# Second FFN of a three-block kernel: rows scaled by their gates as they leave PSUM, added into the residual by the scattering transfer, and one memory-to-memory copy to the output

## The chip, the cores and the metric

The kernel runs on one core of a Trainium2 chip. The metric is the device time of one execution in microseconds, lower is better. A core has TensorE (PE) for matrix products, VectorE (DVE), ScalarE (ACT) and GpSimd (POOL) for elementwise work, and SyncE (SP), which only issues DMAs here. ACT and POOL issue DMAs too. Each engine works through its own list of instructions in order; semaphores tie the lists together. Indirect DMAs, whose rows are picked by a list of row numbers, are issued by POOL, which describes each of their rows.

## The reference

A residual stream x of 2 x 2048 tokens with 256 numbers each passes through an FFN with experts, a Mamba block and the same FFN again:

```
x = L0_attn_x
x = x + 0.5 * _L0_ffn_ref(_layernorm(x, axis=-1), ...)
x = x + _L0_attn_ref(_layernorm(x, axis=-1), ...)
x = x + 0.5 * _L0_ffn_ref(_layernorm(x, axis=-1), ...)
```

The FFN sends each token to the 2 of 8 experts with the largest logits, and adds their outputs weighted by a softmax over these two:

```
logits = jnp.einsum('btd,ed->bte', x, router_w)
top_vals, top_idx = jax.lax.top_k(logits, K)
top_w = jax.nn.softmax(top_vals, axis=-1)
h = jnp.einsum('nd,edh->enh', xf, w1)
h = jnp.square(jax.nn.relu(h))
y = jnp.einsum('enh,ehd->end', h, w2)
y_sel = y[idx_f, jnp.arange(N)[:, None]]
out = jnp.einsum('nk,nkd->nd', w_f, y_sel)
```

Everything is float32; the expert's hidden width is 512.

## The kernel before

The program has three blocks one behind the other: `ffn_block` with `first=True`, `mamba_block`, and `ffn_block` with `first=False`. The Mamba block leaves the residual rows in the tensor `x2_d` and the normalised rows in `xn_d`, both in the chip's memory. Only the third block is changed.

**Routing.** The second FFN has TOK = 4096 tokens, T = 32 groups of P = 128. Every token goes to two experts (TOP = 2), so there are 8192 pairs of a token and an expert. They are sorted by expert, and each expert's part is filled up to a multiple of 128: NT = 72 tiles of 128 rows. DVE makes the tables in a chain of small instructions: `gates` (two weights per token, already halved, L774 and L775), `token_of` (for each row of each tile the token whose normalised row is read, L785), `row_of` (the row of `ys_d` to which the result goes, L788) and `expert_i` (the expert of each tile, L793). The filling rows of a tile go to spare rows behind the real ones (`spare`). `ys_d` has a row for each pair, so no two rows of any tiles meet. While the tables are made, SP loads the low parts of the weights from `lo_d` (L344).

**The tile loop.** For tile t: POOL gathers 128 rows of `xn_d` (L422, tile `xs`); PE turns them (L601), ACT and DVE split them into a high and a low part (L504, L800); PE multiplies by the first weights with three pairs of parts, six products of 512 columns (L613, `pH`); ACT applies the relu (L491); PE turns the result (L622, `pR`), ACT squares it (L497, L499), DVE makes its low part (L805); PE multiplies by the second weights, twelve products (L633, `pY`); DVE copies the 128 x 256 result to `y` (L811, printed as `xs`, since both lie in one tensor), and POOL scatters it to `ys_d` (L427). PE works ahead: in the step of tile t it multiplies tile t+2, turns the rows of tile t+3 and the hidden values of t+1, and then finishes t (`down`). There are NX = 8 buffers for gathered rows and 8 for results.

On POOL the order is: eight gathers, and then in step t the gather for tile t+8 (which waits until PE has turned tile t) and the scatter of tile t (which waits for DVE's copy of tile t):

```
for t in range(NT):
    if t + NX < NT:
        gather(t + NX)
    scatter(t)
```

**The end.** During the tiles SP loads the residual `x2_d` in eight pieces of 512 KB to a tensor in SBUF, `res` (L377; it is printed as `room`). When all scatters have landed, SP loads both rows of every token from `ys_d` (L384, sixteen loads of 512 KB, three buffers), DVE multiplies them by their gates and adds them to `res` (L851, 64 instructions of 128 x 256), and ACT stores the eight finished pieces (L532).

Of the kernel before, what the change touches and what calls it, by code (L numbers as in the profile page):

```python
# [15 lines left out]
P = 128  # L16
D = 256
# [148 lines left out]
def ffn_block(nc, c, keep, x, router_w, w1, w2, xn_d, ys_d, lo_d, out, first, tables=None, early=None):  # L166
# [13 lines left out]
    TOK = x.shape[0]  # L180
# [4 lines left out]
    with ExitStack() as ctx:  # L185
        def sb(name, shape, dt):
            return ctx.enter_context(nc.sbuf_tensor(name, shape, dt))
# [6 lines left out]
        def step(name, unit=1):  # L194
            return Step(sem(name), unit)
# [16 lines left out]
        scratch = Carved(tables if first else sb("room" + tag, [P, T * D], F32))  # L212
        res = None if first else scratch.tensor[:, :].rearrange("p (i d) -> p i d", d=D)
# [32 lines left out]
        er = [a.rearrange("p (r n d) -> p r n d", r=TOP, d=D) for a in (*(xs[:, u * EG * TOP:(u + 1) * EG * TOP, :].rearrange("p n d -> p (n d)") for u in range(2)), hs[:, :])]  # L246
        NE = len(er)
# [33 lines left out]
        e_loaded = [step(f"e_loaded{u}", 16 * TOP) for u in range(NE)]  # L281
        out_loaded, early_loaded, early_hi, early_split = (sem(n) for n in ("out_loaded", "early_loaded", "early_hi", "early_split"))
        res_loaded, e_stored = sem("res_loaded"), sem("e_stored")
        e_first, e_done = step("e_first"), step("e_done")
# [38 lines left out]
        def _(sp):  # L323
# [49 lines left out]
            if out is not None:  # L373
                sp.wait_ge(experts_known, 1)
                for n in range(T // EG):
                    sp.wait_ge(y_copied.sem, y_copied.done(n * NT // (T // EG)))
                    sp.dma_start(res[:, n * EG:(n + 1) * EG, :], tiles(x, n * EG * P)).then_inc(res_loaded, 16)  # L377
                for u in range(NX):
                    sp.wait_ge(scattered[u].sem, scattered[u].done(NT // NX - 1))
                for n in range(T // EG):  # L380
                    if n >= NE:
                        sp.wait_ge(e_done.sem, e_done.done((n - NE + 1) * EG - 1))
                    for k in range(TOP):
                        sp.dma_start(er[n % NE][:, k, :, :], tiles(ys_d, n * EG * P + (1 + k * T) * P)).then_inc(e_loaded[n % NE].sem, 16)  # L384

        @block.gpsimd
        def _(pool):
# [6 lines left out]
            pool.iota(spare[:, :], pattern=[[0, NT // NX], [P, NX]], base=(C + 1) * P, channel_multiplier=1,  # L394
# [30 lines left out]
            def scatter(t):  # L425
                pool.wait_ge(y_copied.sem, y_copied.done(t))
                pool.indirect_dma_start(out=ys_d, out_offset=bass.IndirectOffsetOnAxis(ap=row_of[:, t:t + 1], axis=0),  # L427
                                        in_=y[:, t % NX, :], in_offset=None).then_inc(scattered[t % NX].sem, 16)
# [3 lines left out]
            pool.wait_ge(routed, 2)  # L432
            for t in range(NT):
                if t + NX < NT:
                    gather(t + NX)
                scatter(t)
            for u in range(NX):
                pool.wait_ge(scattered[u].sem, scattered[u].done(NT // NX - 1))

        @block.scalar  # L440
        def _(act):
# [87 lines left out]
            if out is not None:  # L529
                for n in range(T // EG):  # L530
                    act.wait_ge(e_done.sem, e_done.done(n * EG + EG - 1))
                    act.dma_start(tiles(out, n * EG * P), res[:, n * EG:(n + 1) * EG, :]).then_inc(e_stored, 16)  # L532
                act.wait_ge(e_stored, 16 * (T // EG))

# [127 lines left out]
        def _(dve):  # L662
# [112 lines left out]
            link(dve.tensor_tensor(gates[:, T:2 * T], gates[:, 0:T], top[:, 3, :], ALU.mult))  # L775
            dve.wait_ge(oh_used.sem, oh_used.done(C // PC - 1))
# [8 lines left out]
            dve.tensor_scalar(token_of[:, :], row_t[:, :], TOK - 1, None, ALU.bitwise_and).then_inc(routed, 1)  # L785

            link(dve.scalar_tensor_tensor(row_f[:, 2, :], row_f[:, 0, :], 0.0, spare[:, :], ALU.is_equal, ALU.mult))
            dve.tensor_tensor(row_of[:, :], row_f[:, 0, :], row_f[:, 2, :], ALU.add).then_inc(routed, 1)  # L788
# [4 lines left out]
            dve.tensor_scalar(expert_i[:, :], expert_f[:, :], float(E - 1), float(WCOLS), ALU.min, ALU.mult).then_inc(experts_known, 1)  # L793

# [12 lines left out]
            def copy_y(t):  # L807
                dve.wait_ge(y_ready.sem, y_ready.done(t))
                if t >= NX:
                    dve.wait_ge(scattered[t % NX].sem, scattered[t % NX].done(t // NX - 1))  # L810
                dve.tensor_copy(y[:, t % NX, :], pY[t % 2][:, 0:D]).then_inc(y_copied.sem, 1)  # L811
# [27 lines left out]

            if out is not None:  # L840
                for s in (*e_loaded, e_first, e_done):
                    s.open(dve)
                dve.wait_ge(res_loaded, 16 * (T // EG))
                for n in range(T // EG):
                    dve.wait_ge(e_loaded[n % NE].sem, e_loaded[n % NE].done(n // NE))
                    for k in range(TOP):
                        for m in range(EG):
                            i = n * EG + m
                            if k > 0:
                                dve.wait_ge(e_first.sem, e_first.done(i))  # L850
                            dve.scalar_tensor_tensor(res[:, i, :], er[n % NE][:, k, m, :], gates[:, i + k * T:i + k * T + 1], res[:, i, :],  # L851
                                                     ALU.mult, ALU.add).then_inc((e_first, e_done)[k].sem, 1)
# [850 lines left out]
def program(nc, x, w_in, conv_w, conv_b, dt_bias, a_log, d_skip, norm_w, w_out, router_w, w1, w2, out):  # L1703

    with ExitStack() as ctx:
        batches, tokens = x.shape[0], x.shape[0] * x.shape[1]
        xf, of = x.rearrange("b t d -> (b t) d"), out.rearrange("b t d -> (b t) d")

        xn_d = nc.dram_tensor("xn_d", (tokens, D), F32, kind="Internal").ap()
        ys_d = nc.dram_tensor("ys_d", ((TOP * (tokens // P) + 1 + NX) * P, D), F32, kind="Internal").ap()  # L1710
        x2_d = nc.dram_tensor("x2_d", (tokens, D), F32, kind="Internal").ap()
        lo_d = nc.dram_tensor("lo_d", (2, P, E * WCOLS), F32, kind="Internal").ap()
        c = make_constants(nc, ctx)
        keep = make_keep(nc, ctx, tokens)
        build_constants(nc, c)
        with ExitStack() as mid:
            with nc.sbuf_tensor("room1", [P, 4 * WORDS], F32) as tables:
                pass
            early = early_weights(nc, mid, w_in, norm_w, w_out)
            ffn_block(nc, c, keep, xf, router_w, w1, w2, xn_d, ys_d, lo_d, None, True, tables, early)  # L1720
            mamba_block(nc, c, keep, early, xf, ys_d, conv_w, conv_b, dt_bias, a_log, d_skip, x2_d, xn_d, batches)
        ffn_block(nc, c, keep, x2_d, router_w, w1, w2, xn_d, ys_d, lo_d, of, False)
# [24 lines left out]
```

## Time and profile before

| | |
|---|---|
| time, median of 3 runs | 1263.86 us (1262.22 to 1272.66) |
| span of the profiled execution | 1265.8 us |
| PE busy over the span | 1050.3 us (83%) |
| DVE, ACT, POOL busy | 748.1, 605.8, 607.9 us |
| second FFN: tables | about 927 to 965 us |
| second FFN: tiles | about 965 to 1226 us |
| second FFN: combining and storing | about 1226 us to the end |

The span goes from the first to the last instruction of the profiled execution, and it is 1.9 us longer than the median time of the runs. Engines run side by side, so busy times don't add up to the span. What counts is which engine is waited for in a stretch. A row of the chain of waits gives what the program's end waited for, back in time. "Granted clock" is the share of TensorE's full clock that the chip's throttle let it have.

### The profile page before, as it was taken

The page shows a single profiled execution, that of the slowest core. Times are in us where ns is not written, and L with a number is a line of the kernel's source. Part 1 is how long each engine was busy: PE and PEld are TensorE (multiplying, and loading weights), DVE is VectorE, ACT ScalarE, POOL GpSimd, SP SyncE. Part 2 cuts the span into 40 slices and gives each one's busy share as a digit, 9 for nine tenths or more (in the row PEclk, how much of TensorE's full clock was granted, in tenths as well). Part 3 has the DMA queues.
Part 4 walks back from the last instruction along what each step waited for, and adds up shares of the span by engine and source line. Part 5 has one row for each costly group of instructions (what it writes and reads, how often), then busy time and mean ns, then how long its engine had stood idle before and what let it go on. Part 6 is the DMA issues. An engine that isn't in the chain of part 4 may idle for free. (4 is left out here: it accounts for less than half of the span.)

```text
span 1265.8 us, 21732 instructions
## 1 busy us (share of the span) xinstructions
PE 1050.3 (83%) x6532; PEld 870.1 (69%) x6532; DVE 748.1 (59%) x1614; ACT 605.8 (48%) x1560; POOL 607.9 (48%) x612
## 2 busy tenths in 40 slices
PE   3746999999965788989898888989836999999960
PEld 2745999999954556666676666657525999999950
DVE  5974444444427778677878786865355444444437
ACT  1323555555533455556555656565314555555530
POOL 6922555555531245354545454647502555555520
PEclk9997999999985598899989989999858999999985
DMA  7872222322313101111111110000061232222339
GB/s 227 276 294 74 76 76 76 99 76 76 76 59 93 38 30 43 42 42 42 43 42 42 43 38 17 27 17 21 22 279 38 88 97 92 94 95 91 100 117 327
DMA packets 73258, 112.20 MB, mean 89 GB/s; under 512 B 10680, under 2 KB 60352, under 8 KB 71872
## 3 DMA queue, kind: packets, MB, share of 16 engines
q1 hardware_dynamic: 48704, 60.48, 14.2%
q0 software_dynamic: 13824, 37.77, 9.3%
q10 hardware_dynamic: 10624, 12.58, 2.9%
q8 instruction: 61, 1.00, 0.3%
q14 instruction: 45, 0.37, 0.1%
HBM read 66.76 MB, written 44.04 MB: 88 GB/s over the span
## 5 line engine op out<-in xcount | busy, mean ns | idle before, releaser
L427 POOL DMA_INDIRECT ys_d<-xs,row_of x144 | 142.4, 989 | 195.6 <-DVE xs L811 188.2
L422 POOL DMA_INDIRECT xs<-xn_d,token_of x144 | 140.1, 973 | 115.1 <-DVE token_of L785 71.8
L491 ACT ACTIVATE hs<-pH 128x512 f32<-128x512 f32 x144 | 86.0, 597 | 227.6 <-PE pH L613 217.6
L800 DVE TENSOR_TENSOR xl<-pT,xh 128x256 fp32r<-128x256 f32 x144 | 61.1, 424 | 212.7 <-PE pH L613 108.7
L805 DVE TENSOR_TENSOR h2l<-hs,h2h 128x512 fp32r<-128x512 f32 x144 | 99.8, 693 | 81.3 <-ACT h2h L499 77.3
L1604 DVE SCALAR_TENSOR_TENSOR acc<-bank,cwh,acc 128x511 f32<-128x511 f32 (+2 forms) x120 | 89.6, 747 | 40.5 <-ACT acc L1218 37.7
L633 PE MATMUL pY<-w2h,h2h 128*128 x576 | 103.5, 302 | 1.4 <-DVE h2l L805 1.2
L1122 POOL TENSOR_TENSOR yv<-yv,sz 128x512 f32<-128x512 f32 x32 | 40.7, 1272 | 120.6 <-DVE yv L1643 117.4
L613 PE MATMUL pH<-w1h,xh 128*128 x288 | 93.0, 405 | 1.8 <-DVE xl L800 1.1
L613 PE MATMUL pH<-w1l,xh 128*128 x288 | 92.3, 402 | 0.0
L633 PE MATMUL pY<-w2h,h2l 128*128 x576 | 91.1, 280 | 0.0
L613 PE MATMUL pH<-w1h,xl 128*128 x288 | 90.9, 397 | 0.0
L633 PE MATMUL pY<-w2l,h2h 128*128 x576 | 89.5, 278 | 0.0
L497 ACT ACTIVATE hs<-pR 128x512 f32<-128x512 f32 x144 | 87.3, 606 | 4.2 <-PE pR L622 4.2
L499 ACT ACTIVATE h2h<-pR 128x512 fp32r<-128x512 f32 x144 | 89.0, 618 | 0.0
L622 PE MATMUL pR<-ident,hs 128*128 128x128 f32 x576 | 86.3, 272 | 0.0
L633 PEld LDWEIGHTS pY<-w2h,h2h 128*128 128x128 f32 x576 | 78.2, 190 | 2.5 <-issue 2.5
L1106 POOL TENSOR_TENSOR m_rstd<-m_ve,neghalf 128x3 f32<-128x3 f32 x43 | 41.1, 956 | 76.2 <-DVE m_ve L1533 76.2
L633 PEld LDWEIGHTS pY<-w2h,h2l 128*128 128x128 f32 x576 | 77.5, 188 | 0.0
L633 PEld LDWEIGHTS pY<-w2l,h2h 128*128 128x128 f32 x576 | 76.9, 188 | 0.0
L1316 PE MATMUL bank<-wo,yT 128*128 128x256 f32 x256 | 74.0, 440 | 0.0
L1245 ACT ACTIVATE ex<-bank,dts 128x128 f32<-128x128 f32 x256 | 73.3, 380 | 0.6 <-PE bank L1391 0.6
(250 smaller groups left out, 2591.4 us busy)
## 6 DMA issues: line engine op xcount, KB each, us to landing
m_yg<-ys_d SPq DMA_DIRECT2D x64, 128.0 KB, 2.1
xs<-ys_d SPq DMA_DIRECT2D x12, 512.0 KB, 6.8
wst<-in_L_ffn_w_dram ACTq DMA_DIRECT2D x8, 512.0 KB, 4.6
xs<-in_L_attn_x_dram SPq DMA_DIRECT2D x8, 512.0 KB, 6.5
hs<-in_L_ffn_w_dram ACTq DMA_DIRECT2D x8, 512.0 KB, 4.7
xn_d<-xs SPq DMA_DIRECT2D x8, 512.0 KB, 3.4
lo_d<-w1l SPq DMA_DIRECT2D x1, 4096.0 KB, 11.8
lo_d<-w2l SPq DMA_DIRECT2D x1, 4096.0 KB, 21.4
```

The source lines that it names most:

```text
L422: pool.indirect_dma_start(out=xg[:, t % NX, :], out_offset=None, in_=xn_d, in_offset=bass.IndirectOffsetOnAxis(ap=token_of[:, t:t + 1], ax ...
L427: pool.indirect_dma_start(out=ys_d, out_offset=bass.IndirectOffsetOnAxis(ap=row_of[:, t:t + 1], axis=0), in_=y[:, t % NX, :], in_offset=No ...
L491: act.activation(r[:, u, :], pH[u][:, :], ACT.Relu).then_inc(relu_done.sem, 1)
L497: act.activation(h2[:, u, :, :], turned_h, ACT.Square)
L499: act.activation(h2h[:, u, :, :], turned_h, ACT.Square).then_inc(sq_done.sem, 1)
L613: last = pe.matmul(pH[u][:, :], a[:, u, k, :], w[:, k * HID:(k + 1) * HID], start=(n == 0), stop=(n == 3 * KD - 1))
L622: last = pe.transpose(pR[u][:, k * P:(k + 1) * P], r[:, u, k * P:(k + 1) * P], ident[:, :])
L633: last = pe.matmul(pY[u][:, 0:D], a[:, u, k, :], w[:, k * D:(k + 1) * D], start=(n == 0), stop=(n == 3 * KH - 1))
L805: dve.tensor_tensor(h2l[:, u, :, :], h2[:, u, :, :], h2h[:, u, :, :].bitcast(F32), ALU.subtract).then_inc(h2_split.sem, 1)
L1245: last = act.activation(ex[:, i % 2, h, :], pE[:, n * P:(n + 1) * P], ACT.Exp, bias=dts[:, G % 3, NCUM, k * H + h:k * H + h + 1])
L1316: last = pe.matmul(out, a, b, start=(m == 0), stop=(m == len(parts) - 1))
L1604: ins = dve.scalar_tensor_tensor(a, bank[:, 0:GT - n], cwh[:, b, HALO - n:HALO - n + 1], a, ALU.mult, ALU.add)
```

## The change

Only the second FFN (`summed`) does something else:

- DVE multiplies each row of `pY` by its gate as it copies it from PSUM (`tensor_scalar` with a column of `gate_of` in place of `tensor_copy`).
- The scatter has `compute_op=ALU.add` and writes to the residual `x2_d` itself, so both rows of a token end up on one row. `row_of` is now the token's number. The two rows of a token lie in different tiles, and therefore the scatter of tile t waits until the scatter of tile t-1 has landed. `x2_d` gets 1024 spare rows.
- Each tile needs its 128 gates, one per partition. SP stores `gates` to a tensor `gates_d` in memory, DVE computes the place of each row's gate (`gate_at`), and POOL fetches 128 single numbers per tile with an indirect DMA, eight tiles ahead.
- The residual isn't loaded, `ys_d` isn't read, and nothing is combined at the end. When all scatters have landed, SP copies `x2_d` to the output in four pieces of 1 MB, memory to memory.

```diff
-def ffn_block(nc, c, keep, x, router_w, w1, w2, xn_d, ys_d, lo_d, out, first, tables=None, early=None):
-    TOK = x.shape[0]
+def ffn_block(nc, c, keep, x, router_w, w1, w2, xn_d, ys_d, lo_d, out, first, tables=None, early=None, gates_d=None):
...
+    summed = not first
+    TOK = xn_d.shape[0]
...
-        scratch = Carved(tables if first else sb("room" + tag, [P, T * D], F32))
-        res = None if first else scratch.tensor[:, :].rearrange("p (i d) -> p i d", d=D)
+        scratch = Carved(tables if first else sb("room" + tag, [P, 4 * WORDS], F32))
...
-        er = [a.rearrange("p (r n d) -> p r n d", r=TOP, d=D) for a in (*(xs[:, u * EG * TOP:(u + 1) * EG * TOP, :].rearrange("p n d -> p (n d)") for u in range(2)), hs[:, :])]
-        NE = len(er)
+        gate_row = sb("gate_row" + tag, [P, 2, NT], U32) if summed else None
+        gate_at = sb("gate_at" + tag, [P, NT], U32) if summed else None
+        gate_of = sb("gate_of" + tag, [P, NT], F32) if summed else None
...
-        e_loaded = [step(f"e_loaded{u}", 16 * TOP) for u in range(NE)]
-        res_loaded, e_stored = sem("res_loaded"), sem("e_stored")
-        e_first, e_done = step("e_first"), step("e_done")
+        gates_known, gates_stored, gates_found, out_stored = (sem(n) for n in ("gates_known", "gates_stored", "gates_found", "out_stored"))
+        gated = [Step(sem(f"gated{u}"), 16, 0) for u in range(NX)] if summed else []
...
-            if out is not None:
-                sp.wait_ge(experts_known, 1)
-                for n in range(T // EG):
-                    sp.wait_ge(y_copied.sem, y_copied.done(n * NT // (T // EG)))
-                    sp.dma_start(res[:, n * EG:(n + 1) * EG, :], tiles(x, n * EG * P)).then_inc(res_loaded, 16)
+            if summed:
+                sp.wait_ge(gates_known, 1)
+                sp.dma_start(gates_d, gates[:, :]).then_inc(gates_stored, 16)
                 for u in range(NX):
                     sp.wait_ge(scattered[u].sem, scattered[u].done(NT // NX - 1))
-                for n in range(T // EG):
-                    if n >= NE:
-                        sp.wait_ge(e_done.sem, e_done.done((n - NE + 1) * EG - 1))
-                    for k in range(TOP):
-                        sp.dma_start(er[n % NE][:, k, :, :], tiles(ys_d, n * EG * P + (1 + k * T) * P)).then_inc(e_loaded[n % NE].sem, 16)
+                for n in range(NA):
+                    rows = slice(n * TOK // NA, (n + 1) * TOK // NA)
+                    sp.dma_start(out[rows, :].rearrange("(p n) d -> p (n d)", p=P), x[rows, :].rearrange("(p n) d -> p (n d)", p=P)).then_inc(out_stored, 16)
+                sp.wait_ge(out_stored, 16 * NA)
...
-            pool.iota(spare[:, :], pattern=[[0, NT // NX], [P, NX]], base=(C + 1) * P, channel_multiplier=1,
+            pool.iota(spare[:, :], pattern=[[0, NT // NX], [P, NX]], base=P if summed else (C + 1) * P, channel_multiplier=1,
...
             def scatter(t):
                 pool.wait_ge(y_copied.sem, y_copied.done(t))
-                pool.indirect_dma_start(out=ys_d, out_offset=bass.IndirectOffsetOnAxis(ap=row_of[:, t:t + 1], axis=0),
-                                        in_=y[:, t % NX, :], in_offset=None).then_inc(scattered[t % NX].sem, 16)
+                if summed:
+                    if t > 0:
+                        pool.wait_ge(scattered[(t - 1) % NX].sem, scattered[(t - 1) % NX].done((t - 1) // NX))
+                    pool.indirect_dma_start(out=x, out_offset=bass.IndirectOffsetOnAxis(ap=row_of[:, t:t + 1], axis=0),
+                                            in_=y[:, t % NX, :], in_offset=None, compute_op=ALU.add).then_inc(scattered[t % NX].sem, 16)
+                else:
+                    pool.indirect_dma_start(out=ys_d, out_offset=bass.IndirectOffsetOnAxis(ap=row_of[:, t:t + 1], axis=0),
+                                            in_=y[:, t % NX, :], in_offset=None).then_inc(scattered[t % NX].sem, 16)
+
+            def fetch_gate(t):
+                pool.indirect_dma_start(out=gate_of[:, t:t + 1], out_offset=None, in_=gates_d.rearrange("p (c a) -> (p c) a", a=1),
+                                        in_offset=bass.IndirectOffsetOnAxis(ap=gate_at[:, t:t + 1], axis=0)).then_inc(gated[t % NX].sem, 16)
 
             for t in range(NX):
                 gather(t)
             pool.wait_ge(routed, 2)
+            if summed:
+                pool.wait_ge(gates_stored, 16)
+                pool.wait_ge(gates_found, 1)
+                for t in range(NX):
+                    fetch_gate(t)
             for t in range(NT):
                 if t + NX < NT:
                     gather(t + NX)
                 scatter(t)
+                if summed and t + NX < NT:
+                    fetch_gate(t + NX)
             for u in range(NX):
                 pool.wait_ge(scattered[u].sem, scattered[u].done(NT // NX - 1))
...
-            if out is not None:
-                for n in range(T // EG):
-                    act.wait_ge(e_done.sem, e_done.done(n * EG + EG - 1))
-                    act.dma_start(tiles(out, n * EG * P), res[:, n * EG:(n + 1) * EG, :]).then_inc(e_stored, 16)
-                act.wait_ge(e_stored, 16 * (T // EG))
...
+            dve.sem_inc(gates_known, 1)
...
+            if summed:
+                dve.wait_ge(routed, 1)
 
             link(dve.scalar_tensor_tensor(row_f[:, 2, :], row_f[:, 0, :], 0.0, spare[:, :], ALU.is_equal, ALU.mult))
-            dve.tensor_tensor(row_of[:, :], row_f[:, 0, :], row_f[:, 2, :], ALU.add).then_inc(routed, 1)
+            if summed:
+                link(dve.tensor_copy(row_f[:, 1, :], token_of[:, :]))
+            dve.tensor_tensor(row_of[:, :], row_f[:, 1 if summed else 0, :], row_f[:, 2, :], ALU.add).then_inc(routed, 1)
...
+            if summed:
+
+                link(dve.tensor_copy(row_t[:, :], row_f[:, 0, :]))
+                link(dve.tensor_scalar(gate_row[:, 0, :], row_t[:, :], P - 1, None, ALU.bitwise_and))
+                link(dve.tensor_scalar(gate_row[:, 1, :], row_t[:, :], P.bit_length() - 1, None, ALU.logical_shift_right))
+                link(dve.scalar_tensor_tensor(row_f[:, 2, :], gate_row[:, 0, :], float(C), gate_row[:, 1, :], ALU.mult, ALU.add))
+                dve.tensor_scalar(gate_at[:, :], row_f[:, 2, :], -1.0, 0.0, ALU.add, ALU.max).then_inc(gates_found, 1)
...
                 dve.wait_ge(y_ready.sem, y_ready.done(t))
                 if t >= NX:
                     dve.wait_ge(scattered[t % NX].sem, scattered[t % NX].done(t // NX - 1))
-                dve.tensor_copy(y[:, t % NX, :], pY[t % 2][:, 0:D]).then_inc(y_copied.sem, 1)
+                if summed:
+                    dve.wait_ge(gated[t % NX].sem, gated[t % NX].done(t // NX))
+                    dve.tensor_scalar(y[:, t % NX, :], pY[t % 2][:, 0:D], gate_of[:, t:t + 1], None, ALU.mult).then_inc(y_copied.sem, 1)
+                else:
+                    dve.tensor_copy(y[:, t % NX, :], pY[t % 2][:, 0:D]).then_inc(y_copied.sem, 1)
...
-            if out is not None:
-                for s in (*e_loaded, e_first, e_done):
-                    s.open(dve)
-                dve.wait_ge(res_loaded, 16 * (T // EG))
-                for n in range(T // EG):
-                    dve.wait_ge(e_loaded[n % NE].sem, e_loaded[n % NE].done(n // NE))
-                    for k in range(TOP):
-                        for m in range(EG):
-                            i = n * EG + m
-                            if k > 0:
-                                dve.wait_ge(e_first.sem, e_first.done(i))
-                            dve.scalar_tensor_tensor(res[:, i, :], er[n % NE][:, k, m, :], gates[:, i + k * T:i + k * T + 1], res[:, i, :],
-                                                     ALU.mult, ALU.add).then_inc((e_first, e_done)[k].sem, 1)
...
-        x2_d = nc.dram_tensor("x2_d", (tokens, D), F32, kind="Internal").ap()
+        x2_d = nc.dram_tensor("x2_d", (tokens + NX * P, D), F32, kind="Internal").ap()
+        gates_d = nc.dram_tensor("gates_d", (P, TOP * tokens // P), F32, kind="Internal").ap()
...
-        ffn_block(nc, c, keep, x2_d, router_w, w1, w2, xn_d, ys_d, lo_d, of, False)
+        ffn_block(nc, c, keep, x2_d, router_w, w1, w2, xn_d, ys_d, lo_d, of, False, gates_d=gates_d)
```

The instructions in their order show what this moves. On POOL the rows that follow are those of the second FFN from its last table instruction (`spare`) on, of before; `xs<-xn_d,token_of` is a gather, `ys_d<-xs,row_of` a scatter:

```order
L394 IOTA spare 128x72
L422 DMA xs<-xn_d,token_of 128x256 x9
L427 DMA ys_d<-xs,row_of 9344x256
L422 DMA xs<-xn_d,token_of 128x256
L427 DMA ys_d<-xs,row_of 9344x256
L422 DMA xs<-xn_d,token_of 128x256
```

The same place with the change; `gate_of<-gates_d,gate_at` is a fetch of gates, and the scatter is the row with `x_d` (the name under which `x2_d` is printed):

```order
L391 IOTA spare 128x72
L419 DMA xs<-xn_d,token_of 128x256 x8
L434 DMA gate_of<-gates_d,gate_at 128x1 x8
L419 DMA xs<-xn_d,token_of 128x256
L427 DMA x_d<-xs,row_of 5120x256
L434 DMA gate_of<-gates_d,gate_at 128x1
L419 DMA xs<-xn_d,token_of 128x256
L427 DMA x_d<-xs,row_of 5120x256
L434 DMA gate_of<-gates_d,gate_at 128x1
```

Eight fetches stand between the eighth and the ninth gather, ahead of the first scatter, and behind every scatter one more stands ahead of the next gather. The last eight scatters have nothing between them.

On SP, the end of the program as a difference (minus is before, plus is with the change):

```order
 L344 DMA w1l<-lo_d 128x2048
 L344 DMA w2l<-lo_d 128x2048
-L377 DMA room<-x_d 128x4x256 x8
-L384 DMA xs<-ys_d 128x4x256 x4
-L384 DMA hs<-ys_d 128x4x256 x2
-L384 DMA xs<-ys_d 128x4x256 x4
-L384 DMA hs<-ys_d 128x4x256 x2
-L384 DMA xs<-ys_d 128x4x256 x4
-L185 UNCONDITIONAL_BRANCH
+L375 DMA gates_d<-gates 128x64
+L380 DMA out_dram<-x_d 16x16384 x4
```

The eight loads of the residual, which stood beside the tiles, and the sixteen loads behind them are gone; in their place stand one small store ahead of the tiles and four copies behind them.

## Rows read from the trace of the kernel before

**Rows 1.** Spans of the cores: span and mean granted clock.
```profile
core 0: 1265.8 us, clock 0.917
```
**Rows 2.** Busy time by stretch (us, instructions), granted clock, DMA share and rate.
```profile
core 0: us, PE busy (x) PEld busy (x) DVE busy (x) ACT busy (x) POOL busy (x), PEclk, DMA share, GB/s
927.00:965.00 38.00, 15.06 (x195) 13.61 (x195) 29.82 (x66) 11.75 (x25) 2.07 (x4) 0.69 0.54 222
...
981.00:1100.00 119.00, 119.00 (x826) 108.13 (x825) 50.20 (x103) 63.21 (x137) 67.08 (x69) 1.00 0.29 94
1100.00:1217.00 117.00, 117.00 (x814) 106.40 (x813) 50.18 (x102) 62.91 (x136) 61.49 (x63) 1.00 0.28 90
...
1226.00:1266.00 40.00, 0.00 (x0) 0.00 (x0) 25.89 (x64) 0.00 (x0) 0.00 (x0) 0.51 0.92 315
500.00:900.00 400.00, 361.64 (x2002) 264.85 (x2003) 291.58 (x608) 230.08 (x686) 210.16 (x210) 0.95 0.11 34
```
**Rows 3.** One line's instructions, 950 to 1266 us: scatters, gathers (ns min/median/max).
```profile
L427 POOL DMA_INDIRECT ys_d<-xs,row_of x72: 969/987/999, 981.5 to 1224.0; - x72
...
L422 POOL DMA_INDIRECT xs<-xn_d,token_of x72: 942/970/1277, 965.1 to 1197.7; - x72
```
**Rows 4.** Timeline of POOL: start, duration, instruction, [idle before <- its releaser].
```profile
965.08 1.09 POOL L422 DMA_INDIRECT xs<-xn_d,token_of  x1 [35.95 <-DVE token_of L785]
...
975.23 0.95 POOL L422 DMA_INDIRECT xs<-xn_d,token_of  x1 [0.31 <-issue]
981.47 1.00 POOL L427 DMA_INDIRECT ys_d<-xs,row_of  x1 [5.29 <-DVE xs L811]
...
989.02 0.99 POOL L427 DMA_INDIRECT ys_d<-xs,row_of  x1 [1.21 <-DVE xs L811]
990.32 0.97 POOL L422 DMA_INDIRECT xs<-xn_d,token_of  x1 [0.30 <-issue]
992.48 0.99 POOL L427 DMA_INDIRECT ys_d<-xs,row_of  x1 [1.19 <-DVE xs L811]
```
**Rows 5.** Chain that ended last, behind the tiles: start, us, what.
```profile
1224.04 2.37 DMA ys_d<-xs,row_of
...
1226.91 4.69 DMA xs<-ys_d
...
1231.71 6.46 DVE room L851 x16
```
**Rows 6.** Timeline of all engines: the last copy and the last scatter.
```profile
1223.34 0.42 DVE L811 COPY xs<-pY 128x256 f32<-128x256 f32 x1 [1.38 <-PE pY L633]
1224.04 0.97 POOL L427 DMA_INDIRECT ys_d<-xs,row_of  x1 [0.83 <-DVE xs L811]
```
**Rows 7.** Chain that ended last, in the tile stage: start, us, what.
```profile
966.48 2.77 DMA xs<-xn_d,token_of
...
970.69 2.92 PE pH L613 x6
...
1108.70 1.39 PE pH L613 x6
```
**Rows 8.** DMA from 926 to 950 us in 40 slices, only the weight loads.
```profile
GB/s 0 0 14 164 177 382 437 410 396 437 410 437 437 410 423 437 423 423 423 437 423 437 437 437 396 423 437 437 437 423 382 437 437 410 423 437 396 150 14 0
DMA packets 1156, 8.43 MB, mean 351 GB/s; under 512 B 128, under 2 KB 128, under 8 KB 128
```
**Rows 9.** Timeline of DVE: gates, expert numbers, first split of gathered rows.
```profile
961.19 0.19 DVE L775 TENSOR_TENSOR gates<-gates,top 128x32 f32<-128x32 f32 x1
...
964.97 0.23 DVE L788 TENSOR_TENSOR row_of<-row_f 128x72 uint32<-128x72 f32 x1
...
966.69 0.20 DVE L793 TENSOR_SCALAR expert_i<-expert_f 128x72 int32<-128x72 f32 x1
969.24 0.42 DVE L800 TENSOR_TENSOR xl<-pT,xh 128x256 fp32r<-128x256 f32 x1 [2.35 <-ACT xh L504]
```

## The prediction

> **What bounds the kernel now.** I read the table of busy time by stretch first. The second FFN's 72 tiles run between 965 and 1226 us. From 981 to 1217 us PE is busy for the whole of both stretches at a granted clock of 1.00 (2.4 GHz), while POOL is busy for 67 of 119 us [rows 2]. So PE sets the pace there. The distance between two scatters is that pace: 72 of them start between 981.47 and 1224.04 us, and in the steady part they are about 3.45 us apart [rows 4, 6]. Behind the last tile comes a tail in which PE does nothing: from 1226 to 1266 us DVE is busy for 26 of 40 us and the DMA engines for 0.92 of the time, at 315 GB/s [rows 2]. The chain of waits says what that tail is: the last scatter lands 2.37 us after its start, that is at 1226.41, and from there loads of `ys_d` and the combining instructions alternate until the end [rows 5]. The tail from that landing to the end of the span (1265.8 us [rows 1]) is 39.4 us.
>
> Next I read POOL's timeline, because the change gives POOL more to do. An indirect transfer holds POOL for 0.97 us (gather) or 0.99 us (scatter), and the next one never starts earlier than 0.30 us behind it [rows 3, 4]. In the tile loop POOL does a gather and a scatter per tile, 2.56 us with the gaps, and waits for the rest of the 3.45 us: 1.19 or more of idle time stands ahead of the scatter, on DVE's copy.
>
> **The change part by part.** *Removed, tail.* The eight loads of the residual during the tiles, the sixteen loads of `ys_d`, 64 combining instructions and eight stores go. Only the work behind the landing of the last scatter counted: 39.4 us.
>
> *Added, tail.* Four copies of 1 MB each from memory to memory, 4.19 MB. No row shows such a copy. The nearest are the weight loads at this stage's start, 8.4 MB in long runs, which move 437 GB/s at their best and 410 to 437 in most slices [rows 8]: 4.19 MB at 437 is 9.6 us, and about 2 us to start and finish (the scatter's 2.37 is mostly that) makes 11.6 us, the low bound. If every byte counts twice, since it is both read from and written to the memory, it is 19.2 + 2 = 21 us. I take 13, nearer to the row, since a load is also a read and a write of each byte, only to another memory. With 0.1 us for SP to wake, the tail falls from 39.4 to 13.1 us: a gain of 26.3.
>
> *Moved to DVE's tile work.* The copy out of PSUM becomes a multiplication by a gate. The copy takes 0.42 us [rows 6]; DVE is busy for 50 of 119 us [rows 2]. A doubling would still be hidden. It now also waits for its gate, but gates are fetched eight tiles ahead. Six small instructions more on DVE's route to the tables, about 0.23 us each: one of them stands ahead of the expert numbers, which are ready at 966.89 before the first `xh` is available for DVE at 969.24; five behind it end near 968.4 [rows 9]. Hidden, at 0. The store of the gates (SP) starts once the gates are known, near 961.4 [rows 9], and POOL asks for it only at 975: also 0.
>
> *Added on POOL, ahead of the tiles.* POOL's eight first gathers run from 965.08 to the start of a ninth at 975.23, then POOL idles 5.29 us until the first scatter at 981.47 [rows 4]. Now eight fetches of gates stand there. A fetch describes 128 rows like a gather, only of 4 bytes each; I price it like a gather, 0.97 + 0.30, a little less (1.25) in this early part. So the ninth gather starts at 975.2 + 10.0 = 985.2 and the first scatter at 986.5 instead of 981.5. PE doesn't see this yet, its buffers are filled.
>
> *Added on POOL, per tile.* (a) One fetch: POOL's work per tile grows to 0.99 + 0.97 + 0.97 + 3 x 0.30 = 3.83 us, more than PE's 3.45. Even with nothing else, POOL becomes the pace. (b) A wait: scatter t may start only when scatter t-1 has landed. Behind that wait on POOL stand the fetch for tile t+8 and the gather for t+9, on which PE's transposes wait. With a the time from a scatter's start to its landing, scatters start at least a + 0.28 us apart; 0.28 is what POOL takes to start after a releaser (DVE's copy ends at 1223.76, the scatter starts at 1224.04 [rows 6]). The fetch and the gather fit into that time (2.54 us with gaps).
>
> How long is a for an adding scatter? No row shows one. Below, it can't be less than the plain scatter's 2.37 [rows 5], for it writes the same bytes. Above, the old rows of the residual have to be read first, and a gather of 128 rows takes 2.77 us [rows 7]; both in full, one behind the other, make 5.14. Without the second describing (0.97) that is 4.17. I take 3.8, the middle between the ends and a little under 4.17, since reading the two operands overlaps in part. Scatters then start 4.08 us apart, which is over 3.83, so the wait and not POOL's work sets the pace.
>
> *Where the stall goes.* A gather is issued eight tiles ahead of its own scatter, but PE turns tile t+3 before it finishes tile t, so about four tiles of lead remain. POOL starts 5 us late and falls behind by 0.63 us per tile; within some ten to fifteen tiles PE waits for gathered rows on every tile.
>
> **The sum**, against the span of 1265.8. Last scatter starts: 986.5 + 71 x 4.08 = 1276.2 (before: 1224.04), 52.2 later. It lands 1.4 us later after its start than before. Tail: 26.3 less. 1265.8 + 52.2 + 1.4 - 26.3 = 1293.1. The profiled execution's span is 1.9 us above the median of the runs shown (1263.86), so the time is **1291 us**.
>
> **The rivals.**
> *B, the landing is quick and POOL's own work is the pace.* For a up to 3.5, POOL needs 3.83 us for each of 63 steps; the last eight have no gather or fetch and are spaced by a + 0.28. With a = 2.37 and the quick copy: 986.5 + 63 x 3.83 + 8 x 2.65 + 2.4 + 0.1 + 11.6 - 1.9 = 1261. With a = 3.5 and a copy of 13: 1273. All of this is within 1%. For it: 2.37 is measured and adding moves only 128 KB. Against it: the read of the destination isn't in any scatter row.
> The Trainium skill ("DMA: Bandwidth & Descriptors", "Anatomy of one DMA — SWDGE (gpsimd) path") gives about 2.0 us fixed, mostly the receipt of the write, plus bytes at 436 GB/s. For 128 KB that is 2.3, and the trace agrees for the plain scatter with 2.37. "Collectives: The Full Stack" of the Trainium skill (in its account of why ReduceScatter is half of AllGather) says that the addition itself costs nothing and the second source read counts. By both a is about 2.6, an estimate, and the time 1265.
>
> *C, POOL needs longer to describe an adding scatter.* It has two sources per row. If that costs half of an instruction more (0.49 us), the pace is 4.32 and the time 1298; if it costs a whole one more (0.97), 1332. Above 0.19 us more per scatter it is over 1% slower, even with a = 2.37. The gather's and the scatter's near equal rows [rows 3] say that direction doesn't matter and the number of rows does, and that speaks for a moderate surcharge only.
>
> *D, faster.* Here PE stays the pace. The place is the fetch: if it holds POOL for under 0.59 us, POOL's work is at most 3.45 us per tile. With a under 3.17 the last scatter then starts at 1224 as before, the time is 1224 + 2.4 + 13.1 - 1.9 = 1238. It decides up to about 0.8 us with a = 2.37 (1251). For it: the fetch moves 4 bytes per row where the gather moves 1 KB. Against it: POOL's row is the describing of 128 rows, and this doesn't depend on the bytes in any row here; the 144 rows of both kinds lie between 0.94 and 1.28 us [rows 3].
>
> *E, the clock.* PE would be idle in some 15% of each tile. From 500 to 900 us it is busy for 90% at a clock of 0.95; from 927 to 965 us for 40% at 0.69 [rows 2]. A tile's six wide products take 2.92 us at the low level and 1.39 at the full one [rows 7], so a tile at 1.2 GHz takes up to 6.9 us, and PE would then be the pace again. If every tenth tile is such, that is 7 x 2.8 = 20 us more, 1311.
>
> **How the numbers follow.** About 1% is what a measurement of this kernel can tell from no change: 1251.2 and 1276.5. The forecast (the wait for the landing is the pace, a from 3.6 to 5.14, 1277 to 1388, and above 4.55 it is over 1345) has 0.55; B 0.26; C 0.10; E 0.03; D 0.06. So faster 0.06, same 0.26, slower 0.68. The range goes from 1262, B's low end, to 1345, a of 4.55; outside lie D, the edge of B and the forecast's far end, together under 0.2.
>
> **What would show it.** The distance between the starts of two scatters on POOL in mid-stage: 4.1 by the forecast, 3.83 by B, 3.45 by D. What stands ahead of the scatter: by the forecast a wait for the DMA of the scatter before, by B and C nothing but the 0.30. The duration of the adding scatter on POOL: 0.99 by the forecast, 1.5 or 2 by C; that of the fetch: 0.97, under 0.6 by D. PE's transposes of gathered rows should wait for their DMA on most tiles. From the landing of the last scatter to the end: 13 us. The forecast is wrong if the landing takes under 3.5 us or over 4.6, or if the copy takes over 20.

## The result, and the profile after

The changed kernel takes 1343.28 us (median of 4 runs, 1336.46 to 1345.21) against 1268.26 us for the one before in the same runs: 1.059 times as long, interval 1.0546 to 1.0638. The direction was forecast, the size was not: +27 us were forecast, +75 measured.

The columns are those of before. First, busy time by stretch (as [rows 2]), then the adding scatters by their line (as [rows 3]):

```profile
1000.00:1100.00 100.00, 83.46 (x538) 71.73 (x537) 34.15 (x68) 44.37 (x89) 77.11 (x64) 0.97 0.36 56
1100.00:1200.00 100.00, 79.50 (x508) 66.63 (x506) 32.08 (x64) 43.78 (x85) 76.73 (x65) 0.98 0.35 58
...
1325.00:1340.00 15.00, 0.00 (x0) 0.00 (x0) 0.00 (x0) 0.00 (x0) 0.00 (x0) 0.50 0.84 280
...
L427 POOL DMA_INDIRECT x_d<-xs,row_of x72: 1557/1616/2099, 986.3 to 1320.4; - x72
...
DMA to landing us min/median/max: 3.6/3.8/4.4
```

PE, busy throughout before, now stands idle for a fifth of the tile stage; POOL is busy for 77%. The granted clock is 0.97 and 0.98 in the two stretches of the tile stage that are shown. The landing takes 3.8 us, exactly as taken in the sum, but POOL's row for the adding scatter is 1.62 us and not 0.99. POOL's timeline in mid-stage and at the end (as [rows 4]):

```profile
1100.44 1.62 POOL L427 DMA_INDIRECT x_d<-xs,row_of  x1 [0.44 <-DVE xs L833]
1102.36 0.99 POOL L434 DMA_INDIRECT gate_of<-gates_d,gate_at  x1 [0.30 <-issue]
1103.65 0.95 POOL L419 DMA_INDIRECT xs<-xn_d,token_of  x1 [0.30 <-issue]
1105.08 1.62 POOL L427 DMA_INDIRECT x_d<-xs,row_of  x1 [0.47 <-DVE xs L833]
...
1311.58 1.56 POOL L427 DMA_INDIRECT x_d<-xs,row_of  x1 [2.92 <-DMA x_d<-xs,row_of]
1315.96 1.56 POOL L427 DMA_INDIRECT x_d<-xs,row_of  x1 [2.82 <-DMA x_d<-xs,row_of]
```

The median distance of two scatters in mid-stage is 4.59 us. POOL's work alone makes 1.62 + 0.99 + 0.95 + 0.90 = 4.46 of it, so little is left to tell whether work or wait is the pace. (The profile puts the 0.44 down to DVE's copy; that copy is for a tile three or four further on, and the experiments show the real releaser to be the landing.) The chain of waits, at the end where scatters follow each other with nothing between (as [rows 5]):

```profile
1311.58 3.65 DMA x_d<-xs,row_of
1315.22 0.03 issue
1315.25 0.02 POOLq L426
1315.27 0.69 issue
1315.96 3.73 DMA x_d<-xs,row_of
```

From landing to the next start (I call this the restart) go 0.73 us here, where 0.28 was taken from the start behind DVE's copy [rows 6]. In mid-stage the trace has the landing of about two in three scatters, and the median restart behind them is 0.77 us; with the landing's 3.82 that makes the whole distance of 4.59. SP starts the copies at 1324.06, and the span ends at 1339.7.

### The profile page after: what moved, and what is told of

It reads as the page before. It is cut to its first block and busy times, and to the rows that moved or that the text cites. A ratio compares the mean times of both kernels' runs of the same rounds, so it can differ in the third digit from the quotient of the medians.

```text
span 1339.7 us, 21760 instructions
## 1 busy us (share of the span) xinstructions
PE 1063.4 (79%) x6500; PEld 871.0 (65%) x6532; DVE 725.9 (54%) x1556; ACT 617.0 (46%) x1560; POOL 728.2 (54%) x684
## 5 line engine op out<-in xcount | busy, mean ns | idle before, releaser
L427 POOL DMA_INDIRECT x_d<-xs,row_of x72 | 118.5, 1646 | 53.7 <-DMA x_d<-xs,row_of 22.1
L430 POOL DMA_INDIRECT ys_d<-xs,row_of x72 | 71.4, 992 | 98.5 <-DVE xs L835 95.7
L609 PE MATMUL pT<-ident,xs 128*128 128x128 f32 x288 | 59.9, 291 | 68.0 <-DMA xs<-xn_d,token_of 68.0
L609 PEld LDWEIGHTS pT<-ident,xs 128*128 128x128 f32 x288 | 36.3, 143 | 104.6 <-DMA xs<-xn_d,token_of 88.5
L518 ACT ACTIVATE xh<-pT 128x256 fp32r<-128x256 f32 x144 | 54.7, 380 | 67.7 <-PE pT L609 67.7
L434 POOL DMA_INDIRECT gate_of<-gates_d,gate_at x72 | 71.4, 992 | 21.9 <-issue 21.9
## 6 DMA issues: line engine op xcount, KB each, us to landing
lo_d<-w2l SPq DMA_DIRECT2D x1, 4096.0 KB, 21.4
```

The lines of the kernel that those rows point to most:

```text
L427: pool.indirect_dma_start(out=x, out_offset=bass.IndirectOffsetOnAxis(ap=row_of[:, t:t + 1], axis=0), in_=y[:, t % NX, :], in_offset=None, ...
L434: pool.indirect_dma_start(out=gate_of[:, t:t + 1], out_offset=None, in_=gates_d.rearrange("p (c a) -> (p c) a", a=1), in_offset=bass.Indir ...
L609: last = pe.transpose(pT[t % 2][:, k * P:(k + 1) * P], xg[:, t % NX, k * P:(k + 1) * P], ident[:, :])
```

## The experiments

Two theories stood: **W**, POOL's own work is the pace (rival C of the prediction), and **L**, the wait for the landing is. Code ahead of the second FFN is the same in all kernels, but its time isn't: between 400 and 600 us the granted clock was 0.84 in before and in after, 0.94 in `neither`, and the second FFN's first gather started anywhere from 953.7 to 972.0 us (979.6 where its tables were changed). So I compare from that first gather to the end of the span. All numbers (in us) are from POOL's timelines. The distance is the median of the 11th to the 60th, the distance at the end that of the last seven, where only scatters are left. In `preload` and `swap_preload` the last three of these seven stand behind tiles whose rows are all skipped, and are 3.5 us; those before them are 4.4 to 5.1. `before`, `after`, `swap` and `swap_preload` were run several times, the others once; the numbers of the table are of one profiled execution each.

| kernel | gather to first scatter | distance, median | distance at the end | gather to end |
|---|---|---|---|---|
| before | 16.4 | 3.46 | | 300.7 |
| after | 21.5 | 4.59 | 4.53 | 374.9 |
| no_fetch | 15.7 | 4.60 | 4.52 | 366.9 |
| plain_scatter | 21.6 | 3.95 | 3.13 | 321.4 |
| no_wait | 21.6 | 4.47 | 1.87 | 340.8 |
| neither | 15.3 | 3.46 | | 278.2 |
| swap | 21.5 | 4.47 | 4.09 | 358.2 |
| swap_no_fetch | 15.7 | 4.10 | 3.99 | 342.8 |
| extra_wait (half a copy) | 21.4 | 4.58 | 4.51 | |
| preload | 25.8 | 4.70 | 4.45 | 369.0 |
| swap_preload | 25.5 | 4.64 | 4.42 | 364.3 |

**Take the fetches away.** `fetch_gate(t)` isn't called and DVE multiplies by `gates[:, 0:1]`.

> The kernel after without the fetches of gates; every row is scaled by one column of the gates instead, so the output's weights are left out. Theory W (POOL's own work of 4.45 us per tile is the pace: 1.62 + 0.99 + 0.95 and three gaps of 0.30): work falls to 3.16 us, under PE's 3.45, so scatters start 3.45 us apart and the span is about 1224 + 3.8 + 15.6 = 1244 us. Theory L (the wait for the landing of the scatter before is the pace, 3.8 us plus about 0.7 us to start again): scatters stay 4.5 us apart, first at 981.5, span 981.5 + 71 x 4.52 + 3.8 + 15.6 = 1322 us.

1340.65 us, against 1262.56 before. With 1.29 us less work per tile the distance doesn't move; POOL merely waits longer. Its timeline, and then the chain of waits a little further on, in which the restart of 0.77 us can be read between two landings:

```profile
1101.63 1.00 POOL L419 DMA_INDIRECT xs<-xn_d,token_of  x1 [0.30 <-issue]
1104.33 1.58 POOL L427 DMA_INDIRECT x_d<-xs,row_of  x1 [1.69 <-DMA x_d<-xs,row_of]
```

```profile
1099.74 3.81 DMA x_d<-xs,row_of
1103.56 0.02 issue
1103.58 0.02 POOLq L426
1103.60 0.73 issue
1104.33 3.86 DMA x_d<-xs,row_of
```

L holds, and W falls as the pace of the kernel after.

**A plain scatter.**

```diff
-   in_=y[:, t % NX, :], in_offset=None, compute_op=ALU.add)
+   in_=y[:, t % NX, :], in_offset=None)
```

> The kernel after with a plain scatter in place of the adding one; wait and fetches stay, the sum into the residual is left out. Both theories: scatters 3.83 us apart in mid-stage (0.99 + 0.99 + 0.95 + 0.90), last one near 1252, span about 1270. It tells to what the 0.7 us between a landing and the next start belong: if to the adding instruction, the last eight scatters are 2.37 + 0.28 = 2.65 us apart; if to a wait on a DMA, 3.1.

1279.17 us. At the end landings take 2.38 us again, and the distance there is 3.13, so the restart is 0.75 and isn't the addition's. The middle is at 3.95, near POOL's 3.83.

**Take the wait away.** Scatters add to `ys_d`, each row to its own place.

> The kernel after, but the adding scatters go to a row of their own for each pair in the large tensor (as the plain ones did before), so no scatter waits for another; fetches stay; the FFN's part is left out of the output. Theory W: 63 steps of 4.45 us, then eight as fast as PE and POOL allow (about 1.9 to 2.4): last scatter near 1285, span about 1304. Theory L: 3.45 us apart, span about 1244.

1303.01 us, near W's sum. The distance is POOL's work and nothing else:

```profile
1099.34 1.62 POOL L425 DMA_INDIRECT ys_d<-xs,row_of  x1 [0.30 <-issue]
1101.27 0.99 POOL L432 DMA_INDIRECT gate_of<-gates_d,gate_at  x1 [0.30 <-issue]
1102.56 0.96 POOL L419 DMA_INDIRECT xs<-xn_d,token_of  x1 [0.30 <-issue]
1103.82 1.61 POOL L425 DMA_INDIRECT ys_d<-xs,row_of  x1 [0.30 <-issue]
```

So W stands 0.12 us behind L: without the wait the kernel would still lose 40 us against before from the first gather on.

**Neither.** Both edits together.

> Both edits: no fetch and rows of their own without a wait; weights and the FFN's part of the output are left out. Theories W and L both give PE's pace of 3.45 us and a span of about 1244. A third theory (the adding transfers themselves slow the gathers down, so that PE waits for rows) would keep the distance above 4 us.

1233.58 us, and the distance is PE's 3.46 us. The third theory falls: adding transfers don't lengthen the tile stage by themselves.

**The order of the waits, and smaller pieces in the copy.**

```diff
-pool.wait_ge(y_copied.sem, y_copied.done(t))
 if t > 0:
     pool.wait_ge(scattered[(t - 1) % NX].sem, ...)
+pool.wait_ge(y_copied.sem, y_copied.done(t))
```

> The kernel after with two edits that fall in separate stretches. (1) POOL waits first for the landing of the scatter before and then for DVE's copy, instead of the other way round. If the 0.72 us from landing to start come from the last of two waits being on a DMA, the scatters of the last eight tiles go from about 4.5 to about 4.1 us apart; if they belong to any start after a stall on a landing, they stay at 4.5. (2) The final copy goes in rows of 1 KB (4096 pieces) instead of 64 pieces of 64 KB. If the copy is bound by the bytes (read and written at the same memory), it stays near 15.7 us from the last landing to the end; if it is bound by few large pieces, it falls towards 13; if by the number of pieces, it rises.

1314.86 us, and 4.07 at the end as the first guess had it. With rows of 1 KB the tail from the last landing is 16.4 us, where it is 15.7 to 16.1 with pieces of 64 KB (`after`, `no_fetch`, `swap`, `plain_scatter`): the size of the pieces hardly matters. Repeated with the order alone:

> The kernel after with the two waits ahead of the adding scatter in the other order and nothing else. The restart after a landing should take 0.24 us instead of 0.72, so the wait needs 3.8 + 0.24 = 4.05 us per tile and POOL's own work of 4.47 us is the pace; only the last eight stay with the wait, at 4.07. From the first gather to the end: 374.9 - 63 x 0.22 - 8 x 0.5 = 357 us. Time about 1343 - 17 = 1326, 1.046 times before.

1325.84 us (1316.75 to 1330.45, 4 runs) against 1266.9, ratio 1.0447, interval 1.0367 to 1.0526. Now the middle is W's 4.47, and only the end follows the wait:

```profile
1100.14 1.62 POOL L428 DMA_INDIRECT x_d<-xs,row_of  x1 [0.30 <-issue]
1102.06 0.98 POOL L435 DMA_INDIRECT gate_of<-gates_d,gate_at  x1 [0.31 <-issue]
1103.35 0.95 POOL L419 DMA_INDIRECT xs<-xn_d,token_of  x1 [0.30 <-issue]
1104.61 1.62 POOL L428 DMA_INDIRECT x_d<-xs,row_of  x1 [0.30 <-issue]
...
1300.89 1.56 POOL L428 DMA_INDIRECT x_d<-xs,row_of  x1 [2.45 <-DMA x_d<-xs,row_of]
1304.96 1.56 POOL L428 DMA_INDIRECT x_d<-xs,row_of  x1 [2.51 <-DMA x_d<-xs,row_of]
```

> Both the order of the waits changed and the fetches of gates left out (every row is scaled by one column of the gates, the output's weights are left out). Theory L, corrected (landing + restart): 3.8 + 0.24 = 4.05 to 4.1 us per tile throughout, and from the first gather to the end 16.4 + 71 x 4.1 + 19.3 = 327 us, span about 1292. If the pace had been POOL's work alone, the distance would fall to PE's 3.46 and the sum to 281.

1308.71 us; the usual distance is 4.10, as expected, but every fourth one is 5.2 to 6.1 over most of the stage, 16 us in sum. In this kernel all 72 landings are on record. The restart is 0.27 us behind a quick landing and behind most slow ones alike; what is long in the eleven slow distances is the landing itself, 4.9 to 5.8 us instead of 3.8. In each of the eleven a packet of DMA queue 8, which the profile calls `instruction`, starts 2.2 to 3.8 us after the scatter, and no landing without a packet of this queue takes over 4.2 us. For the scatter at 1095.07, which landed after 5.8 us, the queues were:

```profile
q0 software_dynamic: 213, 0.30, 29.9%
q8 instruction: 1, 0.02, 1.0%
```

Such a packet isn't enough alone, since eleven other landings with one beside them are quick. How it delays a landing stays open.

**Why the order matters.** One more wait between the landing's and the scatter, `pool.wait_ge(gates_found, 1)`, and half of the copy.

> The kernel after with two edits in separate stretches. (1) Between the wait for the landing and the adding scatter stands one more wait, on a semaphore that is long satisfied (gates_found); the order of the other two is as in the kernel after. If the restart is short (0.24 us) whenever another wait stands between the landing's wait and the transfer, the last eight scatters are 4.07 us apart and the middle runs at POOL's 4.47; if it needed DVE's wait to stand last for another reason, they stay at 4.5 and 4.6. (2) SP copies only the first half of the residual to the output, 2.1 MB, the second half of the output is left out: with the tail (last landing to end) 15.7 us for 4.2 MB, a copy bound by bytes at 437 GB/s loses 4.8 us, one at 320 GB/s 6.5 us, and the rest, some 3 to 6 us, is fixed.

1326.97 us. The distances stay at 4.51 and 4.58, so it isn't enough that some wait stands between.

The trace shows why, for it has the semaphores of every instruction. Of the waits that the program writes ahead of a scatter, the first one is on the scatter's own instruction, and the others are in an instruction ahead of it. In `after`, `no_fetch`, `plain_scatter` and `extra_wait` the scatter itself waits for DVE's copy, and for the landing waits the instruction ahead (71 of 71 in each); the restart is 0.72 to 0.77 us. In `swap`, `swap_rows` and `swap_no_fetch` it is the other way round (71 of 71), and where the landing sets the pace the restart is 0.26 or 0.27 us. The last scatters show where the difference lies. Their next waits (L452 in `after`, L453 in `swap`) stand behind the scatter in POOL's list. First `after`:

```profile
1319.71 0.02 POOLq L426
1319.73 0.48 issue
1320.21 0.02 POOLq L452
...
1320.42 1.56 POOL x_d L427
```

And `swap`:

```profile
1306.52 2.31 issue
1308.82 0.02 POOLq L453
...
1309.06 1.56 POOL x_d L428
```

From the wait that stands behind the scatter to the scatter's start it is 0.21 and 0.24 us. In `after` 0.50 us pass ahead of that, between the landing's wait (L426) and the one behind the scatter; in `swap` they don't pass behind the landing. So these 0.5 us belong to the scatter's instruction before it waits: they come behind a landing that is waited for ahead of it, and are over by the time of a landing that it waits for itself. What POOL does in them no row says. `extra_wait` put both its waits into the instruction ahead, and so tested less than it was meant to.

The same run prices the copy. The last landing is near 1315.8 and the span ends at 1325.2: 9.4 us for 2.1 MB, 15.7 for 4.2 MB. By these two the copy runs at 2.1 MB / 6.3 us, about 330 GB/s, and some 3.1 us are fixed.

**Fill the output ahead.** `x2_d` is copied to `out` before the tiles, and scatters add to `out`, with filling rows skipped by `bounds_check=TOK - 1, oob_is_err=False`.

> The kernel after, but SP copies the residual to the output ahead of the tiles and the adding scatters go straight to the output (filling rows lie past its end and are skipped). Theory L: the pace stays 4.6 us, the copy's 15.7 us leave the end: span about 1339.7 - 15.7 = 1324. If the skipped filling rows shorten the landing or the output's memory behaves otherwise, the pace changes too.

1333.3 us, span 1331.6. The copy is gone, but from the last scatter's start to the end it is only 10.6 us less: this scatter starts at 1322.94 and, although its landing takes 2.7 us, the span ends 8.7 us later. The first scatter starts 4 us later as well.

> The order of the waits changed and the output filled with the residual ahead of the tiles, so that the adding scatters go to the output itself and no copy is left at the end; the whole output is computed. Pace 4.47 us (POOL's work), no copy: from the first gather to the end 357 - 10.6 = 346 us or a little less, time about 1315, 1.037 times before. It would tell what the form of one residual destination is worth at best with fetched gates.

1328.25 us (1323.63 to 1335.8), ratio 1.0494, interval 1.0412 to 1.0575. Missed: the distance stays at 4.64, and the restart is 0.82 us in mid-stage and 0.77 at the end (`preload`: 0.88 and 0.83). In the chain a POOLq row of the scatter's own line (L425) stands between landing and start, which the kernel `swap` hasn't. It is a MOVE, and the trace shows that with `bounds_check` the landing's wait is on it and no longer on the scatter (71 of 71). The 0.55 us come behind it; the next scatter starts at 1290.67:

```profile
1286.08 3.77 DMA out_dram<-xs,row_of
1289.88 0.03 POOLq L425
1289.91 0.55 issue
```

**An attempt to keep the gain.** Gates are turned into tile order with the tables by PE, and tiles alternate between two destinations:

```diff
+last = pool.tensor_tensor(ohg[:, u, k, :, :], ohhi[:, u, :, :], along(gate_b[:, k, at], NT), ALU.mult)
...
-if t > 0:
-    pool.wait_ge(scattered[(t - 1) % NX].sem, ...)
-pool.indirect_dma_start(out=x, ...
+if t > 1:
+    pool.wait_ge(scattered[(t - 2) % NX].sem, ...)
+pool.indirect_dma_start(out=x[0:TOK, :] if t % 2 else out, ...
```

> No gate fetch and no wait for the scatter just before. The gates are turned with the tables (two more products per item on PE, two more instructions per piece on POOL); even tiles add into the output, which SP fills with zeros ahead, odd ones into the residual, so that a scatter waits for the one two before it; at the end one adding transfer in four pieces brings the residual into the output. Theories L and W both expect PE's pace of 3.46 us (L's distance halves to 2.3, W's work is 3.2 us). Sum from before: 1265.8 - 39.4 (old tail) + 1.4 (slower landing) + 4 (tables) + the adding transfer, which is 12.6 MB of reads and writes: 21 us if the two reads bind, over 32 if all bytes bind. Span about 1253 (1249 to 1266).

1274.34 us against 1272.72 for the kernel before, measured beside it: no gain, and the span of 1272.6 lies outside the expected 1249 to 1266. The tiles run at 3.48 us, and from the first gather to the end it is 293.1 us, 7.6 less than before. But the tables take 56.6 us from the first weight load to the first gather, not 38.0. POOL's new instructions take 1.7 us each, and beside them DVE's of the same size (L803) take up to 1.7 us instead of 0.76, though not every one does. The final adding transfer moves its 4.2 MB at about 205 GB/s.

```profile
943.14 6.87 POOL L419 TENSOR_TENSOR ohg<-room,gate_b 128x576 bf16<-128x576 bf16 x4 [16.32 <-DVE room L803]
...
950.91 0.76 DVE L803 TENSOR_TENSOR room<-room 128x576 bf16<-128x576 bf16 x1 [3.02 <-PE pT L608]
...
961.98 1.63 DVE L803 TENSOR_TENSOR room<-room 128x576 bf16<-128x576 bf16 x1 [1.09 <-PE pT L608]
```

## Why the prediction was right and wrong

The forecast span was 1293.1, the measured one 1339.7, 46.6 more. By the terms of the sum:

- *First scatter at 986.5*: 986.3. Eight fetches ahead of the tiles cost what they were priced at, 1.25 us each.
- *71 distances of 4.08*: 334.1 us instead of 289.7, 44.4 more. This is the term that failed, and in it the restart "a + 0.28". The 0.28 us were read from a start behind DVE's copy, on which the scatter's own instruction waits; behind the landing, for which an instruction ahead of it waits, 0.77 were measured (`plain_scatter`: 0.75 without any addition). That is 71 x 0.49 = 35 us. The landing a was right, 3.82 for 3.8 (1 us); as it was the middle between two bounds far apart, that was in part luck. Single long distances, of up to 7.1 us, add 8; in the longest the landing takes 6.3 us.
- *Landing of the last one*: 0.2 less.
- *Tail of 13.1*: 15.7, 2.6 more. 437 GB/s was read from loads to SBUF; memory to memory it is about 330.

The mechanism of the forecast, that the wait for the landing is the pace, was right, and its own signs of being wrong (a landing under 3.5 or over 4.6, a copy over 20) didn't appear: none of them looked at the restart. But the right restart alone wouldn't have given its time. A second term was too small, POOL's work per tile, 3.83 us with 0.99 for the scatter and 4.47 measured. `swap` has nearly the restart of the forecast, and still takes 1325.84 us.

Rival C was right on its own ground: the adding scatter holds POOL for 1.62 us, 0.63 more, between the two surcharges priced there. It makes a floor of 4.47 us (`no_wait`, `swap`) just under the wait's 4.59, so mending either alone helps little: from the first gather to the end `swap` gains 17 us, no fetch 8, both 32, while neither wait nor fetch gains 97. B is refuted: its 3.83 us needed a scatter of 0.99 and a landing of at most 3.5. With it falls the estimate of 2.6 us that the prediction worked out from "DMA: Bandwidth & Descriptors" of the Trainium skill ("Anatomy of one DMA — SWDGE (gpsimd) path") and the second read: 3.8 were measured. D is refuted by its own term: a fetch of 4 bytes per row takes 0.99 us like a gather of 1 KB. E didn't occur; the granted clock stayed at 0.97 to 0.99 in each 100 us from 1000 to 1300, with PE busy for 80%.

What stays open: what POOL does in the 0.5 us that come behind the landing or ahead of it, why an adding scatter's landing takes 1.4 us more than a plain one's, and how the packets of queue 8 delay some landings.

## What to carry to other kernels

A transfer that must wait for the one before it has a period of landing plus restart, and the restart has to be read from a start behind the same kind of wait. Where two waits stand ahead of an indirect transfer, write the one first that ends last: here the first was the one on the transfer itself, and behind it the restart was 0.5 us shorter. With `bounds_check` this gained next to nothing. An adding scatter doesn't save a pass for free: it takes the engine that describes it 1.6 times as long as a plain one and serialises tiles that may meet, and here the 72 steps grew by 97 us in sum (259 from the first gather to the last scatter before, 356 after) to shorten a tail of 39 to 16. Before work is put on an engine with 1.2 us free per step, sum its rows with their gaps.

## What the hardware showed unexpectedly

- An adding indirect scatter of 128 rows of 1 KB holds POOL for 1.62 us (plain: 0.99) and lands 3.8 us after its start (plain: 2.4). Where all its rows lie past the bound and are skipped, it lands after 2.7.
- The restart behind a landing was 0.73 to 0.77 us when an instruction ahead of the indirect transfer waited for it, and 0.26 to 0.27 us when the transfer itself did; the order of two waits in the program decides which.
- Landings of adding scatters took 4.9 to 5.8 us instead of 3.8 in eleven cases of `swap_no_fetch`, each with a packet of the `instruction` queue 8 beside it.
- A memory-to-memory copy ran at about 330 GB/s with 3.1 us fixed, hardly slower in 1 KB pieces than in 64 KB; an adding one at about 205 GB/s.
- When the program's last transfers were POOL's own, the span ended 4.3 (`two_dest`) or 6.2 us (`preload`, `swap_preload`) after their last packet, and 1.2 us after the last packet in every other kernel.
